# Attention with a window of 32 keys: VectorE's order within a tile of 128 tokens

## The reference, cut to what matters

```python
H, W = 16, 32                      # heads, window; HD = D // H = 8
qkv = layernorm(x) @ Wqkv.T + bqkv
scores = jnp.einsum('bhid,bhjd->bhij', q, k) / jnp.sqrt(HD)
mask = (j <= i) & (j >= i - (W - 1))
probs = jax.nn.softmax(jnp.where(mask, scores, -jnp.inf), axis=-1)
y = jnp.einsum('bhij,bhjd->bhid', probs, v)
x = x + (y.reshape(b, t, d) @ Wo.T + bo)
```

## Time and profile before

| | us |
|---|---|
| median of 3 runs (lowest to highest) | 2192.49 (2189.72 to 2193.07) |
| span of the profiled execution | 2192.3 |
| TensorE busy over the span | 2035.4 |
| VectorE busy over the span | 1491.3 |
| from 100 to 150 us (attention): TensorE, VectorE, ScalarE, GpSimd busy of 50 | 46.30, 36.20, 32.89, 35.53 |

### The profile page before, as it was taken

One profiled execution on the slowest core, in us unless ns is written; L12 is line 12 of the kernel. 1 busy time (PEld: TensorE's weight loads), 2 busy tenths in 40 slices (PEclk: granted clock), 3 DMA queues, 4 the chain that ended last, 5 costly groups with the idle time before them and its releaser, 6 DMA issues. The chain is left out here.

```text
span 2192.3 us, 42562 instructions
## 1 busy us (share of the span) xinstructions
PE 2035.4 (93%) x14462; PEld 1549.4 (71%) x14463; DVE 1491.3 (68%) x2745; ACT 1192.8 (54%) x2383; POOL 1439.4 (66%) x972
## 2 busy tenths in 40 slices
PE   7998999999999989888888889888789999999998
PEld 5776546999999636556565556555554489999994
DVE  6776584333333469999999999999976833333335
ACT  5665322222222259999998898888833232222222
POOL 6775004676767329999999999998940057677660
PEclk9999999999999989999999999999899999999999
DMA  8000100000000422323322222333233000000004
GB/s 299 1 0 1 39 1 14 25 24 24 26 23 25 114 76 98 98 88 102 103 91 96 90 101 93 98 93 93 88 137 140 2 22 24 25 24 25 24 23 119
DMA packets 72343, 141.93 MB, mean 65 GB/s; under 512 B 9979, under 2 KB 43773, under 8 KB 70054
## 3 DMA queue, kind: packets, MB, share of 16 engines
q1 hardware_dynamic: 63142, 121.87, 16.8%
q0 software_dynamic: 9088, 18.63, 2.9%
HBM read 123.82 MB, written 16.65 MB: 64 GB/s over the span
## 5 line engine op out<-in xcount | busy, mean ns | idle before, releaser
L2198 POOL TENSOR_TENSOR m_seen<-m_state,experts 128x1024 f32<-128x1024 f32 x256 | 599.7, 2364 | 62.7 <-DVE m_state L2252 55.3
L2252 DVE TENSOR_TENSOR_SCAN m_state<-experts,ps 128x512 f32<-128x512 f32 x448 | 539.7, 1234 | 0.6 <-PE ps L1789 0.5
L1806 PE MATMUL ps<-ident,m_seen 128*128 128x128 f32 x2048 | 280.7, 282 | 36.6 <-POOL m_seen L2198 36.6
L1806 PEld LDWEIGHTS ps<-ident,m_seen 128*128 128x128 f32 x2048 | 245.0, 145 | 75.4 <-POOL m_seen L2198 55.2
L2011 ACT ACTIVATE experts<-delta,experts 128x512 f32<-128x512 f32 x448 | 291.3, 713 | 1.0 <-DVE delta L2278 0.5
L1520 POOL COPY f_weights<-experts 128x1898 f32 x142 | 252.3, 1777 | 23.8 <-issue 23.5
L1350 PE MATMUL ps<-zu,f_weights 128*128 128x128 f32 x1988 | 242.8, 276 | 2.8 <-issue 1.0
L1350 PE MATMUL first_up_ps<-f_xT,f_weights 128*128 128x128 f32 x1988 | 242.8, 276 | 2.7 <-issue 1.2
L1350 PEld LDWEIGHTS ps<-zu,f_weights 128*128 128x128 f32 x1988 | 233.1, 192 | 6.5 <-issue 5.5
L1350 PEld LDWEIGHTS first_up_ps<-f_xT,f_weights 128*128 128x128 f32 x1988 | 233.1, 192 | 6.5 <-issue 5.6
L2232 DVE TENSOR_TENSOR ps<-m_delta_u,ps 128x512 f32<-128x512 f32 x286 | 193.2, 675 | 19.1 <-PE ps L1764 18.7
(11 more groups left out here) (421 smaller groups left out, 3917.3 us busy)
## 6 DMA issues: line engine op xcount, KB each, us to landing
experts<-m_rows SPq DMA_DIRECT2D x144, 512.0 KB, 3.7
experts<-in_experts SPq DMA_DIRECT2D x17, 1461.0 KB, 19.2
tokens<-f_rows SPq DMA_DIRECT2D x8, 512.0 KB, 5.1
f_rows<-expert_out SPq DMA_DIRECT2D x8, 512.0 KB, 7.0
f_cols<-expert_out SPq DMA_DIRECT2D x8, 512.0 KB, 7.2
out<-X SPq DMA_DIRECT2D x4, 512.0 KB, 3.2
X<-in_x SPq DMA_DIRECT2D x4, 448.0 KB, 5.7
f_xin<-tokens,f_take POOLq DMA_INDIRECT x71, 2.6
```

The costliest lines, as they stand in the source:

```text
L1806: mm = pe.matmul(Y[:, i // 2, at:at + P], seen[:, n % SEEN, h, i * P:(i + 1) * P], ident[:], is_transpose=True, start=(n == 0 and at == 0) ...
L2198: pool.tensor_tensor(seen[:, n % SEEN], state[:, n % RING], c_rep[:, Q % C_RING, n % C_GROUP, :].unsqueeze(1).to_broadcast([P, HALF, SEG]) ...
L2252: dve.tensor_tensor_scan(state[:, n % RING, h, :], decay_, drive_, before_, ALU.mult, ALU.add).then_inc(s_state, 1)
```

## The change

Within a tile VectorE issues its six steps in another order. Before: sum into X, next mask, row statistics, maxima, picking, copy of the turned rows. After: next mask, sum into X, maxima, picking, row statistics, copy of the turned rows. Nothing is added or removed; every wait stays with its step; the other engines' programs and VectorE's `tail` are as before.

```diff
 def body(n, r):
-    if alive(n, r - 2):
-        add_out(at(n, r - 2), tile(n, r - 2)[0], y_ps)
     if alive(n, r + 1):
         add_mask(at(n, r + 1), (r + 1) % 2)
     if alive(n, r - 2):
-        sums_of(at(n, r - 2), tile(n, r - 2)[0])
+        add_out(at(n, r - 2), tile(n, r - 2)[0], y_ps)
     if alive(n, r + 1):
         tops(at(n, r + 1), (r + 1) % 2)
     if alive(n, r - 1):
         pick(at(n, r - 1), y_ps)
+    if alive(n, r - 2):
+        sums_of(at(n, r - 2), tile(n, r - 2)[0])
+    if alive(n, r - 1):
         copy_y(at(n, r - 1), y_ps)
```

## The result

The kernel after takes 2197.49 us in the median of 9 runs (2191.28 to 2201.33), the kernel before 2193.07 us in 9 (2189.63 to 2196.42). The ratio is 1.0024, with a 95% interval of 1.0012 to 1.0035: slower by 4.4 us, where the working had +5.15. The middle of the interval lies just beyond the 0.2% that was named as the bound, its lower end within it.

A forecast was written before the change was run, and what follows sets the result against it. Attention tiles were taken as bound by a ring through VectorE, then by TensorE's order; 1.8 + 0.95 + 1.1 + 1.3 = +5.15 us on the 2192.3 span gave 2197.45, with 0.2 for the median 2197.7, range 2191.5 to 2206.

The forecast's parts named there:

- The ring: Attention tile: before, set through VectorE; after, by TensorE's order of scores, mask, sum, second half of products, the rest.
- The lateness of TensorE: Second half of products waits for the later sum, so TensorE runs 0.65 us late per loop tile, 0.62 unrolled.
- The room: TensorE's idle time before the turning of `y`: 0.56 us a loop tile, 0.43 unrolled, that it can be late for free.
- Loop: Twenty loop tiles, each longer by 0.65 less 0.56, or 0.09 us: +1.8 us.
- Unrolled tiles: Five regular tiles, one ahead of the loop and four behind, each 0.19 us longer: +0.95 us.
- The two small groups: Two tiles with small statistics instructions: the sum comes 1.13 us later, costing +1.1 in the first and +1.3 in the second.
- the 0.8 that I had charged: Second small-statistics tile: 0.8 us for a possible clock fall after its wait grows to 1.77 us.
- The case with the restart 0.1 sooner: TensorE's products restart 0.1 us sooner after the sum: +2.5 us in all, 2195.0, at small odds, counted with Rival 1.
- Rival 1: Mask starts at 1.00, so TensorE's idle time covers the lateness: no change, +0.75 us, 2193.2; chance 0.29.
- Rival 2: Clock falls in ordinary tiles, one in three losing 1.4 us: much slower, 2209 us; chance 0.12.
- Rival 3: Products not held up, VectorE's ring wins: tiles of 5.3 us, 0.5 less each, 2182 us; chance 0.07.
- The statistics behind the picking: Row statistics, 0.28 us, before the copy of turned rows, which waits anyway: no cost; 0.2 a tile without that cover.

The follow-up runs named there:

- E3: The kernel after with the mask cut into two half-size instructions and the sum between them: 0.9965 of before, 2183.57 us.
- e5: The kernel after with the maxima in two instructions of eight heads each and the sum between them: 1.0145 of before, 2223.80 us.
- E1: The kernel before with only mask and sum exchanged, so the row statistics stay between sum and maxima: 1.0031 of before, 2198.86 us.
- e7: The kernel of E3 with the mask cut at a quarter instead of at half: 0.9970 of before, 2185.11 us.
- E2: The kernel before with only the row statistics moved behind the picking: 0.9989 of before, 2190.66 us.
- E4: The kernel after with the sum moved behind all the maxima: 1.0444 of before, 2291.18 us.
- e6: The kernel after with the small statistics instructions ahead of the row statistics and the copy in two tiles: 1.0033 of before, 2198.13 us.

## Why the prediction was right, and where its sizes were off

**The ring.** Predicted behind the turning of `y`: scores 0.23, mask 1.16, sum 2.29, L671 at 3.6, next turning at 5.94. Measured in the tile shown: 0.20, 1.10, 2.24, 3.59, 5.98. The sum's release of the products took 137.56 - 137.15 = 0.41 us in the loop, against the 0.34 of the earlier trace rows; the 0.03 that I had added for the loop was in no row, and 0.07 is what the tile shows. The lateness of TensorE was 0.64 against 0.65: the mask came 0.06 sooner than worked out, and the later release took that back. The room was 0.51 against the 0.56 taken from the idle weight loads (from L671 to the next turning 2.39 us, before 2.90). E3 and e5 confirm by intervention that the sum's place is the cause: moved 0.52 us to the front and 0.7 to the back, it takes the tile with it by 0.52 and 0.73. E1 shows that the place of the statistics has no part in it, and e7 that it ends where TensorE no longer waits for the sum.

**Loop: +0.98 us for +1.8.** Twenty tiles took 119.56 us before and 120.54 after. The ordinary tile grew by 0.13, more than the 0.09. But the turn of the loop shrank, which the prediction had not looked at: before, each turn cost 0.48 us (6.34 instead of 5.86), after, two tiles of a turn take 6.05 to 6.10 instead of 5.98, 0.2 in all. So the +0.98 is two misses of opposite sign: some +2.6 from the ordinary growth of twenty tiles, and some -1.6 at the turns. Scores behind the turning of `y` at a turn, before, then after, then in e1:

```profile
92.85 0.30 PE L713 MATMUL y_ps<-ident,y 128*128 128x128 f32 x1 [0.36 <-DVE y L566]
93.55 0.73 PE L648 MATMUL first_up_ps<-k_spread,qT 32*32 32x256 f32 x32 [0.40 <-issue]
```

```profile
92.65 0.27 PE L714 MATMUL y_ps<-ident,y 128*128 128x128 f32 x1
92.97 0.73 PE L649 MATMUL first_up_ps<-k_spread,qT 32*32 32x256 f32 x32
```

```profile
92.94 0.27 PE L714 MATMUL y_ps<-ident,y 128*128 128x128 f32 x1
93.34 0.73 PE L649 MATMUL first_up_ps<-k_spread,qT 32*32 32x256 f32 x32
```

Before, TensorE waited for `y`, and the scores started 0.70 us behind the turning. After, `y` is there 0.57 us ahead, and the distance is 0.28 to 0.32. E2 and e3, where the turning starts 0.15 and 0.17 us behind the end of the picking, that is as soon as `y` lets it, have 0.70 to 0.72 and 0.67 to 0.70, and pay almost the full price (6.28 against 5.80; 5.92 against 5.46, with a further 0.1 in the next tile). E1 shows the readiness of `y` nearly by itself, since only the place of the statistics differs: its ordinary tile is that of the kernel after, but `y` is there only 0.47 us ahead, the distance is 0.38 to 0.53, and the twenty tiles take 0.5 us more. That it is the loop's branch and register work that is covered meanwhile stays argued.

**Unrolled tiles: +0.80 us for +0.95.** The three full intervals behind the loop grew by 0.25 each (17.93 for 17.19), the one into them by 0.11, and the one ahead of the loop shrank by 0.05, since before it still had a fallen clock in it. The last one in front of `tail`, which I had not counted, shrank from 5.72 to 5.40 us.

**The two small groups: +1.27 and +0.60 us for +1.1 and +1.3.** The mechanism is as described, with the mask in the sum's place. In the profiled execution the clock did not fall behind the second wait of 1.86 us, so the 0.8 that I had charged for it was not paid there; e1, with 2.04 us at the same place, paid 1.5. Over many runs something between is likely, and it is not measured.

**The sum.** 0.98 + 0.80 + 1.27 + 0.60 - 0.32 = +3.33 us, as the stretch shows (+3.32), against +5.15; the timed difference of 4.4 us has an interval of 2.6 to 7.7 (0.12% and 0.35%) and can't part them. That the median came out at 2197.49 where 2197.7 was forecast is in part luck: the terms were 1.8 us too large together, and the kernel before has a median of 2193.07 in these runs where the forecast was built on 2192.49. The stated range also took in no change, so lying inside it says little; it is the sign, the waits and the places of the steps in the trace that bear the mechanism out. The case with the restart 0.1 sooner (+2.5) lies nearer to +3.3 in size, but not in mechanism: the release was later than worked out, not sooner, and in the kernel after weight load and product again start together behind the wait (137.55 and 137.56).

**The rivals.** Rival 1 needed the mask 0.16 sooner; it came 0.06 sooner and the room was 0.05 smaller. Rival 2 did not come: from 45 to 165 us the clock was 1.00. E4 and e5 show how far off it was: waits of 0.5 us in each tile left the clock alone, with 1.2 it fell in five of the tiles behind the first small group, with 1.8 it was low for more than half of the time. Rival 3 needed a sum that does not hold the products; e3 built just that and found 5.46 us a tile where rival 3 had said 5.3.

**The statistics behind the picking** cost nothing, as said. In the ordinary tile they gain nothing either, by e1 (TensorE sets the tile) and e2 (0.06 us, not 0.2, where VectorE sets it); at the turns of the loop and in the last tile their new place gains some 0.7 us together, by e1, which the prediction did not have.

## What to carry to other kernels

When an order is changed to shorten one engine's ring, follow each moved instruction to what it releases elsewhere: here a short sum of 0.28 us was put behind a mask that holds it for 1.13, and the sum, not the mask, was what the other engine needed. Cutting the long instruction in two and putting the short one in the cut gave both engines here what they wait for. A gap between two dependent instructions is a place to put small independent work at almost no price (here 0.06 us for an instruction of 0.28). And a change of a few microseconds in one stage must be read in that stage, from its own first to its own last instruction, as the spans here went the other way.

## What the runs showed of the hardware that I had not expected

- A dependent VectorE instruction started 1.25 us behind the start of a 1.22 us mask, an independent one 1.13: 0.12 us between the two.
- Tiny VectorE instructions (four columns, 0.15 us) took 1.18 and 1.35 us when they met a long GpSimd instruction, and ended with it, within 0.03 us. In the kernel after one of them took 1.18 too, and in the kernel before one took 1.22. The cause is not tested apart.
- Whether the clock falls behind a wait is not told by the wait alone: it fell behind 1.02 us (before) and 2.04 (e1), and not behind 1.86 at the same place (after); in e6 it fell behind 2.30 and not behind 2.33.
- The price of a turn of the loop in TensorE's program went from 0.48 to 0.2 us when the operand awaited at its end came early, and lay between the two (some 0.3) when it came 0.1 us less early (e1).
